# Latent attention: the softmax's sums are taken by GpSimd adds and one PE group instead of a column of ones in V, and the V products run four tiles at a time

## The reference, cut to what matters

```
h = jnp.concatenate([x, latents], axis=1)          # context, then latents
q = (latents @ q_w + q_b).reshape(b, k_len, NH, DH)
kv = (h @ kv_w + kv_b).reshape(b, p + k_len, NH, DH, 2)
attn = jnp.einsum('bkhd,bnhd->bhkn', q, kmat) / DH
attn = jax.nn.softmax(jnp.where(full_mask, attn, -jnp.inf), axis=-1)
attn_out = jnp.einsum('bhkn,bnhd->bkhd', attn, v) @ out_w + out_b + residual
```

## Time and profile before

| | |
|---|---|
| median of 3 runs | 4391.94 us (4382.46 to 4394.99) |
| profiled execution, its own time | 4386.62 us |
| its span | 4384.8 us |
| PE busy | 3985.0 us (91%) |
| DVE, ACT, POOL busy | 2591.4, 1861.2, 1221.3 us |
| granted TensorE clock, mean | 0.963 |

### The profile page before, as it was taken

One profiled execution on the slowest core, in us unless ns is written; L12 is line 12 of the kernel. 1 busy time (PEld: TensorE's weight loads), 2 busy tenths in 40 slices (PEclk: granted clock), 3 DMA queues, 4 the chain that ended last, 5 costly groups with the idle time before them and its releaser, 6 DMA issues. The chain is left out here.

```text
span 4384.8 us, 55237 instructions
## 1 busy us (share of the span) xinstructions
PE 3985.0 (91%) x21018; PEld 2964.1 (68%) x21018; DVE 2591.4 (59%) x4130; ACT 1861.2 (42%) x3286; POOL 1221.3 (28%) x1326
## 2 busy tenths in 40 slices
PE   6899699997999989998878996999979999899988
PEld 5655488886888877543665554888868888775436
DVE  2588655566555665455535885565666556654555
ACT  2487344343434431455124883443434344314541
POOL 1543222132213313221215422131322223131213
PEclk9999799998999999999998997999989999999999
DMA  1211111111101102221222111010111011132212
GB/s 69 61 35 24 39 37 34 32 39 34 37 22 44 39 29 87 54 58 29 80 77 67 36 18 47 29 44 22 39 34 37 22 44 39 39 90 48 51 29 89
DMA packets 167573, 195.62 MB, mean 45 GB/s; under 512 B 18627, under 2 KB 123272, under 8 KB 167310
## 3 DMA queue, kind: packets, MB, share of 16 engines
q1 hardware_dynamic: 142734, 151.15, 11.2%
q0 software_dynamic: 24576, 40.94, 4.8%
HBM read 149.02 MB, written 2.10 MB: 34 GB/s over the span
## 5 line engine op out<-in xcount | busy, mean ns | idle before, releaser
L1293 DVE TENSOR_TENSOR w_pt_lo<-ps,w_pt_hi 128x512 fp32r<-128x512 f32 x512 | 334.8, 685 | 154.1 <-ACT w_pt_hi L1227 154.1
L1082 POOL CAST w_wo_hi<-w_raw 128x1024 fp32r<-128x1024 f32 x32 | 34.1, 1065 | 1323.2 <-PE ps L148 1323.2
L1227 ACT ACTIVATE w_pt_hi<-ps 128x512 fp32r<-128x512 f32 x512 | 281.3, 595 | 200.5 <-PE ps L1161 200.5
L897 DVE CUSTOM_DVE_ANT_0 g_units<-ps,g_mask 128x1024 f32<-128x1024 f32 x256 | 311.1, 1217 | 81.4 <-PE ps L760 81.3
L1700 ACT ACTIVATE h_pt<-ps,zero_col 128x512 f32<-128x512 f32 x384 | 257.1, 686 | 231.8 <-PE ps L1656 230.3
L1749 DVE TENSOR_REDUCE h_mxs<-ps 128x1 f32<-128x512 f32 x384 | 243.6, 684 | 161.6 <-PE ps L1645 159.9
L1276 DVE TENSOR_REDUCE w_mx<-ps 128x1 f32<-128x1024 f32 x256 | 311.9, 1218 | 31.5 <-PE ps L148 31.5
L1161 PE MATMUL ps<-ident,w_p 128*128 128x128 f32 x2048 | 279.1, 275 | 39.4 <-DVE w_pt_lo L1293 39.4
L772 PE MATMUL ps<-ident,g_units 128*128 128x128 f32 x2048 | 291.2, 283 | 20.2 <-ACT g_turned L851 18.0
L843 ACT ACTIVATE g_units<-g_units,g_nmx 128x1024 f32<-128x1024 f32 x256 | 294.6, 1151 | 17.9 <-DVE g_nmx L897 15.1
L1161 PEld LDWEIGHTS ps<-ident,w_p 128*128 128x128 f32 x2048 | 235.4, 140 | 95.9 <-DVE w_pt_lo L1293 66.5
(11 more groups left out here) (357 smaller groups left out, 10265.3 us busy)
## 6 DMA issues: line engine op xcount, KB each, us to landing
w_raw<-in_L_xattn_wk SPq DMA_DIRECT2D x32, 512.0 KB, 3.4
w_raw<-in_L_xattn_wq SPq DMA_DIRECT2D x32, 512.0 KB, 3.5
w_raw<-in_L_xattn_wv SPq DMA_DIRECT2D x32, 512.0 KB, 3.6
w_raw<-in_L_xattn_wo SPq DMA_DIRECT2D x32, 512.0 KB, 3.6
mlp_raw<-in_L_xattn_w_fc SPq DMA_DIRECT2D x64, 256.0 KB, 3.1
mlp_raw<-in_L_xattn_mlp_w SPq DMA_DIRECT2D x64, 256.0 KB, 3.2
h_ks<-h_k_hi POOLq DMA_DIRECT2D x64, 192.0 KB, 3.0
g_qs<-g_q_hi POOLq DMA_DIRECT2D x256, 32.0 KB, 1.9
```

Source lines behind the costliest of these rows:

```text
L897: dve.tensor_tensor_reduce(units[:, q % U, :].rearrange("p (h w) -> p h w", h=2), ps[:, 2 * (q % 2):2 * (q % 2) + 2, :], mask[:, q % 4, :] ...
L1227: act.activation(pt.h[:, x[2] % 4, :], ps[:, T_BANK + tn % 2, :], ACT.Copy).then_inc(t_hi, 1)
L1293: dve.tensor_tensor(pt.l[:, x[2] % 4, :], ps[:, T_BANK + tn % 2, :], as_f32(pt.h[:, x[2] % 4, :]), ALU.subtract).then_inc(t_free, 1)
```

## The change

- V loses its column of ones and its padding; `vd` is [128, 12, 512].
- `pe_pv` now multiplies four tiles in one group, each by 128 x 32 of V, into the four quarters of the PSUM rows: three groups per head, at j = 5, j = 9 and at j = 1 of the next iteration.
- `pool_z`, new: GpSimd adds tiles 0 to 8 of `pt` into `zs`, eight adds, each waiting for the tile's exponential and for the add before.
- `pe_z`, new, at j = 3 of the next iteration: a group of four products with a 128 x 32 matrix of ones sums `zs` and tiles 9, 10 and 11 into `M_BANK`, which `pe_rows` also uses. ACT copies it to `zparts` at j = 4, and "zq" (now at j = 6) works from there.
- ACT's exponential of tile j in the next head also waits until GpSimd (tiles 0 to 8) or PE (9 to 11) has read the old one.
- GpSimd's loop has one more turn, and in each turn `pool_z(n-1)` comes first. The product a32 shares its tile with the reciprocal, and the mask and output bias share theirs with `zparts` and `zs`.

```
-            S_IN, PV_AT, TAIL = (2, 1, 2, 2, 2, 1, 2), {2 * i + 3: (i,) for i in range(KT // 2 - 1)}, 2
-            PAIRS, PV_LATE = KT // 2, (KT // 2 - 1,)
+            S_IN, PV_AT, TAIL = (2, 1, 2, 2, 2, 1, 2), {5: 0, 9: 1}, 2
...
-                    put(("zq", c - 1), [((n0, 4), ())], (n0, 8))
+                    put(("zq", c - 1), [((n0, 6), ())], (n0, 8))
...
+            def pool_z(pool, b, hd):
+                n, sum_ = b * HEADS + hd, zs[:, hd % 2, :]
+                upto(pool, z_full, n - 1)
+                pool.wait_ge(e_done, n * KT + 2)
+                pool.tensor_tensor(sum_, pt[:, 0, :], pt[:, 1, :], ALU.add).then_inc(z_pool, 1)
+                for i in range(2, SUMMED):
+                    pool.wait_ge(e_done, n * KT + i + 1)
+                    pool.wait_ge(z_pool, n * (SUMMED - 1) + i - 1)
+                    pool.tensor_tensor(sum_, sum_, pt[:, i, :], ALU.add).then_inc(z_pool, 1)
...
-                for n in range(HEADS):
+                for n in range(HEADS + 1):
+                    if n:
+                        pool_z(pool, b, n - 1)
                     if n + 2 < HEADS and (n + 2) % U:
                         spread(pool, b, n + 2)
...
-            def pe_pv(pe, b, hd, pair):
+            def pe_pv(pe, b, hd, i_):
                 n = b * HEADS + hd
-                pe.wait_ge(e_done, n * KT + 2 * pair + 2)
-                if pair == 0:
+                pe.wait_ge(e_done, n * KT + 4 * i_ + 4)
+                if i_ == 0:
                     upto(pe, o_free, n)
-                for j in range(2):
-                    i = pe.matmul(ps[64 * j:64 * j + 64, O_BANK, :], v_and_one(2 * pair + j, hd),
-                                  pt[:, 2 * pair + j, :], start=pair == 0, stop=pair == PAIRS - 1, skip_group_check=True)
+                for j in range(4):
+                    st = 4 * i_ + j
+                    i = pe.matmul(ps[32 * j:32 * j + 32, O_BANK, :], vd[:, st, hd * DH:(hd + 1) * DH],
+                                  pt[:, st, :], start=i_ == 0, stop=i_ == 2, skip_group_check=True)
                 i.then_inc(pv_done, 1)
+
+            def pe_z(pe, b, hd):
+                n = b * HEADS + hd
+                pe.wait_ge(z_pool, (n + 1) * (SUMMED - 1))
+                for j, tile in enumerate([zs[:, hd % 2, :]] + [pt[:, i, :] for i in range(SUMMED, KT)]):
+                    i = pe.matmul(ps[DH * j:DH * j + DH, M_BANK, :], ones_32[:, :], tile,
+                                  start=True, stop=True, skip_group_check=True)
+                i.then_inc(z_full, 1)
...
                         if j == 1 and 0 <= n - 1 < HEADS:
-                            for pair in PV_LATE:
-                                pe_pv(pe, b, n - 1, pair)
+                            pe_pv(pe, b, n - 1, 2)
+                        if j == 3 and 0 <= n - 1 < HEADS:
+                            pe_z(pe, b, n - 1)
...
                             if n:
-                                act.wait_ge(pv_done, (m - 1) * PAIRS + j // 2 + 1)
+                                act.wait_ge(pv_done, (m - 1) * 3 + j // 4 + 1)
+                                if j < SUMMED:
+                                    act.wait_ge(z_pool, (m - 1) * (SUMMED - 1) + max(j, 1))
+                                else:
+                                    act.wait_ge(z_full, m)
```

More of the change, by code:

```diff
@@ L1360, in latent @@
             parts = sb(own, tag + "_parts", [P, U, NQ])
-            mask_i, brow = sb(own, tag + "_mask_int", [P, NK], I32), sb(own, tag + "_bo", [P, D])
+            first = ExitStack()
+            mask_i = sb(first, tag + "_mask_int", [P, NK], I32)
+            brow = sb(first, tag + "_bo", [P, D])
+            first.close()
+            zparts, zs = sb(own, tag + "_zparts", [P, U, NQ]), sb(own, tag + "_zs", [P, 2, NQ])
             kd = Pair(own, tag + "_k", [P, KEYS])
@@ L1365, in latent @@
             raw = sb(own, tag + "_raw", [P, 2, 1024])
-            rzb, a32, att = sb(own, tag + "_rzb", [P, NQ]), sb(own, tag + "_a32", [P, NQ]), Pair(own, tag + "_att", [P, NQ])
+            rzb, att = sb(own, tag + "_rzb", [P, NQ]), Pair(own, tag + "_att", [P, NQ])
+            a32 = rzb
             mxs, mx = sb(own, tag + "_mxs", [P, 2, LT, HF]), sb(own, tag + "_mx", [P, 2, LT])
@@ L1555, in pool_ @@
                 split_raw(pool, b, ("q", 0))
-                for j in (0, 2 * DH):
+                for j in range(0, P, DH):
                     pool.tensor_tensor(folds[:, 0, :], folds[:, 0, :], ident[:, j:j + DH], ALU.add)
-                    pool.tensor_tensor(folds[:, 1, :], folds[:, 1, :], ident[:, DH + j:DH + j + 1].broadcast_to([P, DH]),
-                                       ALU.add)
+                    pool.tensor_tensor(folds[:, 1, :], folds[:, 1, :], ident[:, j:j + 1].broadcast_to([P, DH]), ALU.add)
                     pool.drain()
@@ L1597, in pe_ring @@
                         i = mm3(pe, ring(x), lines_of(k, x[1]), wv[:, k, :], k == 0, k == KC - 1)
-                elif x[0] in ("zq", "fold"):
+                elif x[0] == "zq":
+                    pe.wait_ge(z_out, (g + 1) * U)
+                    for u in range(U):
+                        i = pe.matmul(ring(x)[DH * u:DH * u + DH, :], folds[:, 1, :], zparts[:, u, :],
+                                      start=True, stop=True, skip_group_check=True)
+                elif x[0] == "fold":
                     pe.wait_ge(o_free, (g + 1) * U)
                     for u in range(U):
-                        i = pe.matmul(ring(x)[DH * u:DH * u + DH, :], folds[:, int(x[0] == "zq"), :], parts[:, u, :],
+                        i = pe.matmul(ring(x)[DH * u:DH * u + DH, :], folds[:, 0, :], parts[:, u, :],
                                       start=True, stop=True, skip_group_check=True)
@@ L1657, in pe_ @@
                                       start=True, stop=True, skip_group_check=True).then_inc(st_full, 1)
-                            for pair in PV_AT.get(j, ()):
-                                pe_pv(pe, b, n, pair)
+                            if j in PV_AT:
+                                pe_pv(pe, b, n, PV_AT[j])
                         for x, ks_of in slices.get((n, j), []):
@@ L1679, in act_ring @@
                     ring_wait(act, b, x)
-                    act.activation(v_of(x[1]), by_head(ring(x)), ACT.Copy).then_inc(v_out[x[1] % 2], 1)
+                    act.activation(vd[:, x[1], :], ring(x), ACT.Copy).then_inc(v_out[x[1] % 2], 1)
                 elif x[0] == "fold":
```

29 lines of the change are left out of this document (15 added, 14 removed).

## The result

The changed kernel takes 4405.2 us (median of 6 runs, 4404.0 to 4406.4) against 4387.9 (6 runs, 4382.5 to 4395.0): ratio 1.0038, 95% interval 1.0025 to 1.0050. So it is slower, by 17 us (11 to 22). The forecast was 11.3 us slower, and 4403 us.

The account below looks back on a forecast made before the run. PE was taken as nearly full (busy 268 of 287 us), GpSimd nearly empty. Per batch, gains of 16.55 us less losses of 22.2 made 5.65 slower, 11.3 in two; from the median 4391.9 this gave 4403 us, range 4376 to 4426.

Parts of the forecast that it names:

- PE's saving: Latent stage's head loop: six PE groups per head become four, 2.0 us less PE work each; 16.55 us per batch gained.
- The turns: Iterations 3, 7, 11: adds queued behind the next chunk's spread; PE stands 4.4 us, clock adds 1.3 each, 17.1 per batch.
- the reciprocal's wait: Iterations 4, 8, 12: PE waits before "fold", which takes up savings made before it; only 1.0 us each gained.
- the bare iteration: Iteration 13, without projections or ring jobs: tiles then go at ACT's pace through two PSUM banks; 1.15 us gained, not 2.0.
- Four tiles for the price of two: PE's V groups: four column tiles cost 1.00 us, like two; rival that they don't run at once: 64 us slower, 1 in 20.
- The adds: GpSimd's eight adds per head: a pitch of 1.40 us each, 11.2 us per head.
- The bounds 1.27 and 1.51: Limits in us for the pitch of GpSimd's adds: no gap at all, or the longest add with the drain's gap.
- GpSimd as the bound throughout: Rival, whole head loop: at an add pitch of 1.5 or more lag no longer heals; 25 to 40 us slower, 2 in 10.
- the only meeting: DVE's low part of `att`, once per chunk, alone would contend with an add; the sum stays the same.
- Head 13 and the tail: Late adds: 1.8 us wait for head 13's sum; last head 2.4 us late, 3.3 with the clock.
- The slack: PE asks for the sum 4.0 us into the next iteration, which carries late adds in iterations 4, 5, 8, 9.
- The rival that PE's saving comes through: Whole loop: with add pitch 1.27 and the clock holding, a batch gains 20.4, loses 11.5; 18 us faster, 2 in 10.

Follow-up runs that it names:

- one_add: The changed kernel with one of the eight GpSimd adds per head kept, PE and ACT instructions unchanged: 4355.77 us, 0.9927 of the kernel before.
- turn_order: The changed kernel with five of head n's eight adds put ahead of the next chunk's spread at the three chunk turns: 4376.21 us, 0.9970 of the kernel before.
- turn_split12: turn_order with the split of the third output weights moved from turn 13 to turn 12 of GpSimd's loop: 4379.53 us, 0.9974 of the kernel before.

## Why the prediction was right

**PE's saving.** Forecast 16.55 us per batch; one_add shows 17.5 and 15.4 for the same iterations in its two batches. The sum was right, its shares less so. Iterations 0, 1, 5, 9 gained 8.5 and 5.4 (7.5 forecast); what differs is iteration 9 with its falls of the clock in either kernel. The turns, 2, 6, 10 with 3, 7, 11, gained 1.8 and 2.7 (3.3). Iterations 4, 8, 12 gained 6.5 in both where I had 3.0: the reciprocal's wait didn't swallow the group ahead of it, PE's idle before "fold" fell from 1.43 to 0.66 us. Iteration 13 gained 0.2, not 1.15, and 14 gained 0.6, not 1.6. The times of my walk through the bare iteration hold: counted from the rows group that opens it, it put the V group of j = 9 at 12.69 us and the next score product at 14.89, and in the changed kernel they start at 12.72 and 14.74. What it missed is that the iteration now begins earlier, its first score product 0.78 us behind that rows group instead of 1.88, and that slots 0 to 6, which were to stay as they were, take that much longer. The share of one iteration shows up in the one before it.

**Four tiles for the price of two.** PE in the changed kernel: two tiles' products and the next score product.

```profile
1858.51 1.07 PE L1640 MATMUL ps<-h_pt,h_vd 128*32 128x512 f32 x8
1859.51 0.74 PE L1666 MATMUL ps<-h_ks,h_qs 97*128 97x512 f32 x2
```

Eight records, 1.00 us from start to start, as the earlier trace rows. That rival falls. The Trainium skill, "TensorE: Matmul & The Clock Gate", section "Measured speedup vs the span model", has three column tiles at 2.38 times the speed of one after the other; that four cost here what two cost goes the same way.

**The adds.** By source line, durations min/median/max in ns of the seven in-place ones, both batches:

```profile
L1546 POOL TENSOR_TENSOR h_zs<-h_zs,h_pt x224: 1261/1281/1817, 1799.7 to 4269.2; 128x512 f32<-128x512 f32 x112
```

Seven in 9.74 us plus the gap before them, (1851.72 - 1840.54) / 8: a pitch of 1.40, as forecast; in the row itself 1.41 (9.74 less one of 1.28, by 6). The bounds 1.27 and 1.51 held, and GpSimd as the bound throughout fell with them: with a median of 1281 ns beside DVE's work the adds are as fast as those of the earlier trace rows. By the Trainium skill's "SBUF — State Buffer", section "Who interferes with whom", a DVE instruction with two inputs in SBUF contends with a GpSimd instruction that reads SBUF. The trace agrees: the four longest adds, 1.74 to 1.82 us, are those that start within 0.15 us behind the low part of `att`.

The prediction took this for the only meeting, once per chunk, and left its sum the same with and without it. That was a term put at nothing which wasn't. The adds meet `dve_negate` as well, on tiles of 128 x 4: in 23 of the 30 iterations of both batches one of its instructions takes longer than before. Its negation in one_add and in the changed kernel, min/median/max in ns:

```profile
L1784 DVE TENSOR_SCALAR h_nmx<-h_mx x32: 170/172/173, 1789.9 to 4201.0; 128x4 fp32r<-128x4 f32 x32
...
L1788 DVE TENSOR_SCALAR h_nmx<-h_mx x32: 170/342/1150, 1792.1 to 4250.2; 128x4 fp32r<-128x4 f32 x32
```

Mostly there is time to spare until PE's rows group. In iterations 4, 8, 12 the reciprocal stands right behind it on DVE and "fold" behind that.

**The turns.** 4.4 us of standing and 1.3 of clock for each, 17.1 in a batch. Against one_add, iterations 3, 7, 11 lose 15.0 (16.0 in the second batch). The sum is close and its two parts are not: PE stood for 7.8 us (2.84 + 0.94 + 4.00; 9.5 in the second batch), not 13.2. The other 7.2 us, where I had 3.9, are what is left over. The trace has the clock for them, 0.79, 0.84 and 0.85 in these iterations against one_add's 0.91, 1.00 and 0.90, but no run measures it apart. That the clock falls at such waits I took from the tail of before; that it also falls ahead of the group, behind the wait for the spread's DMAs, I had not counted. That first fall isn't the adds' doing: one_add has it too, 0.50 from 1842 to 1844 us.

**Head 13 and the tail.** Iterations 13 and 14 lost 3.1 and, in the second batch, 1.9 against one_add (1.8 forecast as a wait for the adds). But PE stood for the adds only 0.51 us, and not at all in the second batch, so the number fits and the mechanism doesn't; the clock was 0.91 in iteration 14 and 0.89 in iteration 13 of the second batch. The tail of the changed kernel, PE with ACT and DVE:

```profile
2069.19 9.77 POOL L1546 TENSOR_TENSOR h_zs<-h_zs,h_pt 128x512 f32<-128x512 f32 x7
2079.02 0.62 PE L1648 MATMUL ps<-h_zs,ones 128*32 128x512 f32 x1 [2.04 <-POOL h_zs L1546]
2080.40 0.60 ACT L1739 ACTIVATE h_zparts<-ps 128x512 f32<-128x512 f32 x1 [2.76 <-PE ps L1648]
2081.14 1.94 PE L1606 MATMUL ps<-h_zparts,h_folds 128*32 128x512 f32 x8 [0.79 <-ACT h_zparts L1739]
2083.14 3.36 DVE L1763 RECIPROCAL h_rzb<-ps 128x512 f32<-128x512 f32 x1 [18.79 <-PE ps L1606]
```

Adds until 2078.96, the sum group behind 2.04 us of idle, the copy, and "zq" at half the clock (1.94 instead of 1.07). From the last head's first transposed scores (2064.69, where I counted from 2059.09) the reciprocal starts 18.5 us in, against 14.75 before; I had 17.0, with the clock not in it. From the last rows group to the next norm the tail took 37.4 us against 34.2: 3.2 more, 3.3 forecast.

**The slack** of 4.0 us did carry heads 4, 5, 8 and 9: none of their groups waited. Iterations 4, 8, 12 still lose 2.5 and 3.1 against one_add, which I had not counted. The larger part is the negation held up by an add: in the first batch it takes 0.56, 1.13 and 0.38 us instead of 0.17, and the reciprocal starts later by as much, 0.40, 0.95 and 0.22 us. In the second batch it is 2.2 of the 3.1. In iteration 8 the clock then falls to 0.50 behind the wait for "fold".

**The balance.** 22.2 us forecast as lost per batch, 24.5 and 23.6 measured against one_add (21.0 and 20.1 in the loop, 3.5 in each tail), against 17.9 and 15.7 gained with the tail. That leaves 6.6 and 7.9 per batch where I had 5.65: 14.5 us, not 11.3. The profiled execution is 18.2 us up: these 14.5, 3.3 less in the preparation and 7.0 more outside the stage, and neither of the last two is shown to be the change's. By the medians it is 17. That 4403 and 4405.2 lie so close has luck in it: I started from a median of 4391.9, and over six runs the kernel before has 4387.9.

**The rival that PE's saving comes through** was refuted by the order of the queue, as its "against" said, and turn_order comes near making it true: 0.9970 with all adds in place.

## What to carry to other kernels

Before giving an idle engine new work, look at what its in-order queue waits for: here 330 us of adds would have fitted beside PE, and most of what they cost was decided by a wait for a copy ahead of them. Move the new work ahead of such a wait, or the waiting instruction to a queue with nothing behind it, and only then give the consumer more slack; slack alone hands the lag on until a place that has none. An experiment that leaves the new work out and keeps everything else (one_add) tells saving and cost apart in one run. And compare the durations of the other engines' short instructions with and without the new work: the adds themselves kept their 1281 ns, while a DVE instruction of 0.17 us took up to 1.15 beside them.

## What the runs showed of the hardware

PE's clock decides more here than any one wait. Behind a wait, for the adds, for a spread's DMAs or for DVE's maxima, it often fell from 1.00 (2.4 GHz) to 0.50 (1.2 GHz) and stood there while PE was busy all the time, as in turn_split12 from 4062 to 4066 us; this in kernels with late adds and without. At some places it changes from one batch to the next, and at iteration 5 of turn_split12 the 1.1 us more that PE waited went with the change. With the adds it is more frequent: 0.94 for the loop, where one_add with the same instructions on PE has 0.99.

Some DVE instructions on SBUF did not run beside a GpSimd add. The low part of `att` takes 0.75 us and an add 1.28; where the two met, either DVE took up to 1.87 or the add up to 1.83. The negation of 128 x 4 took 0.17 us in all 32 of one_add and 0.17 to 1.15 in the changed kernel. DVE's maxima, which read PSUM, kept their 0.68 us, and so did the reduction of 128 x 12 ahead of the negation, which reads SBUF, its 0.165 to 0.168.

A semaphore wait between dependent adds on GpSimd costs no more than the drain of the earlier trace rows: 0.13 us beside 0.15. Six DMAs per head issued by SP or by GpSimd make no difference to the time by themselves that the runs could tell (0.9994, 0.9985 to 1.0003).
